# Selective scan: the product with B made in token-by-channel form and turned into PSUM, the states summed by accumulating transposes

## The reference, cut to what matters

```
xz = Z @ in_proj_w.T; x, z = split(xz)                 # 256 channels each
x = silu(causal_conv(x) + b)
dt, B, C = split(x @ x_proj_w.T)                       # 8, 16, 16 columns
dt = softplus(dt @ dt_proj_w.T + dt_proj_b)
h_t = exp(dt_t * A) * h_(t-1) + dt_t * B_t * x_t       # per channel (256) and state (16)
y_t = sum over the 16 states of h_t * C_t,  then y = (y + x * D) * silu(z)
```

## Time and profile before

| | us |
|---|---|
| median of 3 runs (1807.96 to 1814.98) | 1811.38 |
| the profiled execution, its own time | 1805.02 |
| its span in the profile | 1803.2 |
| first scan starts, last gate ends | 161.2, 943.5 |
| PE / DVE / ACT / POOL busy over the span | 1457.0 / 1317.4 / 796.5 / 563.6 |

### The profile page before, as it was taken

How to read it: one execution, slowest core, us unless ns; L and a number is a source line. 1 busy time by engine, 2 the same in 40 slices (tenths; PEclk the granted TensorE clock), 3 DMA queues, 4 the chain that set the end, 5 groups by cost and what they waited for, 6 DMA issues and landing times. The chain is left out here.

```text
span 1803.2 us, 20461 instructions
## 1 busy us (share of the span) xinstructions
PE 1457.0 (81%) x6865; PEld 867.1 (48%) x6866; DVE 1317.4 (73%) x2521; ACT 796.5 (44%) x1946; POOL 563.6 (31%) x460
## 2 busy tenths in 40 slices
PE   3897888887977775798996694412899999999998
PEld 2442333333322222366676563301576767777776
DVE  3607999999999989999980835698355555677667
ACT  4435545453555544344432365520444444444542
POOL 0006535322576652444453741000111110254100
PEclk9997989898888886899998798556899999999999
DMA  5002434344333311234455310101212111012001
GB/s 187 1 1 61 129 93 133 89 114 118 89 102 108 103 59 42 85 111 111 115 135 166 106 29 7 50 0 46 60 40 64 40 39 39 22 35 34 10 7 42
DMA packets 75998, 127.23 MB, mean 71 GB/s; under 512 B 11870, under 2 KB 38718, under 8 KB 75286
## 3 DMA queue, kind: packets, MB, share of 16 engines
q1 hardware_dynamic: 56438, 75.04, 13.8%
q0 software_dynamic: 19456, 50.88, 10.7%
HBM read 85.51 MB, written 40.37 MB: 70 GB/s over the span
## 5 line engine op out<-in xcount | busy, mean ns | idle before, releaser
L539 DVE TENSOR_TENSOR_SCAN sc_st<-sc_dA,sc_st 128x1024 f32<-128x1024 f32 x128 | 291.5, 2318 | 0.0
L1862 DVE COPY at_pT<-at_p_t 128x512 f32<-128x512 f32 (+1 forms) x192 | 109.6, 599 | 174.1 <-PE at_p_t L1756 174.1
L1143 POOL DMA_INDIRECT g_state<-xn_scratch,moe_tab x96 | 123.5, 1286 | 252.4 <-POOLq L194 141.3
L510 DVE TENSOR_TENSOR sc_st<-sc_p_b,sc_u 128x512 f32<-128x512 f32 x256 | 165.6, 682 | 41.6 <-PE sc_p_y L419 31.0
L351 ACT ACTIVATE sc_dA<-sc_dt,g_state 128x511 f32<-128x511 f32 x256 | 169.0, 709 | 27.6 <-DVE sc_st L539 26.1
L1735 PE MATMUL at_p_s<-att_xaT,at_qT 128*128 128x512 f32 (+3 forms) x512 | 173.3, 460 | 0.0
L1769 PEld LDWEIGHTS at_p_o<-at_V,at_pT 128*128 128x128 f32 x1280 | 154.0, 194 | 29.6 <-issue 28.8
L1814 ACT ACTIVATE at_pr<-at_p_s,at_nmx 128x512 f32<-128x512 f32 (+3 forms) x256 | 131.5, 529 | 64.0 <-DVE at_nmx L1840 63.9
L1174 POOL DMA_INDIRECT g_state<-r_scratch,moe_tab x96 | 114.0, 1188 | 141.6 <-PE e_bank L1273 102.0
L400 PE MATMUL sc_p_b<-sc_bc,mamba_sel 96*128 96x512 bf16 x128 | 55.6, 434 | 126.0 <-DVE sc_st L510 125.2
L1769 PE MATMUL at_p_o<-at_V,at_pT 128*128 128x128 f32 x1280 | 155.3, 277 | 1.8 <-DVE g_state L1853 1.8
(11 more groups left out here) (283 smaller groups left out, 2823.2 us busy)
## 6 DMA issues: line engine op xcount, KB each, us to landing
y_scratch<-g_state SPq DMA_DIRECT2D x24, 768.0 KB, 5.4
g_state<-W SPq DMA_DIRECT2D x48, 256.0 KB, 5.4
r_scratch<-g_state SPq DMA_DIRECT2D x16, 512.0 KB, 2.9
y_scratch<-g_state SPq DMA_DIRECT2D x24, 192.0 KB, 3.2
xn_scratch<-g_state SPq DMA_DIRECT2D x16, 256.0 KB, 2.0
g_state<-x SPq DMA_DIRECT2D x4, 512.0 KB, 5.3
g_state<-xn_scratch SPq DMA_DIRECT2D x8, 256.0 KB, 6.0
g_state<-x SPq DMA_DIRECT2D x1, 2048.0 KB, 11.6
```

The source lines that it names most:

```text
L510: ins = nc.vector.tensor_tensor(st[:, m % RS, j, :], p_b[:, :], u[:, b % 2, h, :], ALU.mult)
L539: nc.vector.tensor_tensor_scan(st[:, m % RS, :, :].rearrange("p a b -> p (a b)"), dA[:, m % 4, :, :].rearrange("p a b -> p (a b)"), st[:, ...
L1143: nc.gpsimd.indirect_dma_start(out=self.xg[:, e % 4, h, :], out_offset=None, in_=self.xn_rows, in_offset=bass.IndirectOffsetOnAxis(ap=r.ta ...
```

## The change

Per state instead of per pair (128 iterations N of `n` = 0 to 15 in `b`), with these parts:

- B is computed token by token (`b_by_token`) and u is turned (`turn_u`), so that u and B lie as tokens x channels: B is then one number per partition. `times_b` is a product with a per-partition scalar, 128x256 for each of 4 blocks of tokens: two on ACT, two on DVE, SBUF to SBUF.
- `turn_bu`: TensorE turns the 8 blocks of 128x128 into `p_u` in PSUM, one bank per half. The scans (128x512, two per state) read `p_u` there.
- `add_state`: 8 transposes (`is_transpose`, `start=False`) accumulate the finished state in `p_y`, now tokens x channels. `start_y` puts x * D there first, by products with a diagonal of D.
- `gate` is one product of 128x1024; z comes as tokens x channels from the input stage, and `turn_y` and `take_yT` turn the result back. The ReLU goes from DVE to ACT. `broadcast_b` is gone, and the work of `split_bc` and `softplus` is spread over the iterations.

The core of the diff, in the order input stage, ScalarE (from the ReLU to `take_yT`), TensorE (from `turn_bu` to the two `turn_y` at the end), VectorE:

```diff
-                    nc.scalar.activation(zT[:, e - HALF, b * L:(b + 1) * L], pj[:, n % 3, :],
+                    t = b * TB + 2 * (e - HALF)
+                    nc.scalar.activation(z[:, t:t + 2, :].rearrange("p a b -> p (a b)"), pj[:, n % 3, :],
...
+                link(nc.scalar.activation(logs[:, 1, :], logs[:, 0, :], ACT.Ln, bias=1.0))
+                nc.scalar.activation(dt[:, b % 2, h, :], p_x[:, :], ACT.Relu,
+                                     bias=w["dt_b"][:, h:h + 1]).then_inc(logs_ready, 1)
...
+            def times_b(N):
+                b, n = divmod(N, DS)
...
+                if N >= 3:
+                    act.wait_ge(bu_turned[1], N - 2)
+                for t in range(2):
+                    ins = nc.scalar.activation(bu[:, N % 3, t, :], uT[:, b % 2, t, :], ACT.Copy,
+                                               scale=BT[:, b % 2, t, n:n + 1])
+                ins.then_inc(bu_act, 1)
...
+            for N in range(STATES):
+                b, n = divmod(N, DS)
+                if N + 2 < STATES:
+                    decays(N + 2)
+                yield
+                if N + 2 < STATES:
+                    times_b(N + 2)
+                if b + 1 < B:
+                    if n == 1:
+                        softplus_logs(b + 1, 0)
+                    if n == 4:
+                        softplus_logs(b + 1, 1)
+                    if n == 6:
+                        take_BT(b + 1)
+                    if n == 7:
+                        take_uT(b + 1, 0)
+                    if n == 10:
+                        take_uT(b + 1, 1)
+                if b and n in (11, 12):
+                    take_yT(b - 1, n - 11)
...
+            def turn_bu(N, h):
+                if h == 0:
+                    pe.wait_ge(bu_act, N + 1)
+                    pe.wait_ge(bu_dve, N + 1)
+                if N:
+                    pe.wait_ge(scanned[h], N)
+                for t in range(TB):
+                    ins = nc.tensor.transpose(p_u[:, h, t * P:(t + 1) * P], bu[:, N % 3, t, h * P:(h + 1) * P],
+                                              w["ident"])
+                ins.then_inc(bu_turned[h], 1)
...
+            def add_state(N):
...
+                pe.wait_ge(hc_ready, N + 1)
+                for t in range(TB):
+                    for h in range(HALF):
+                        ins = nc.tensor.matmul(p_y[:, t, h * P:(h + 1) * P], st[:, N % 3, h, t * P:(t + 1) * P],
+                                               w["ident"], is_transpose=True, start=False,
...
+            for N in range(STATES):
+                b, n = divmod(N, DS)
+                if N + 1 < STATES:
+                    turn_bu(N + 1, 0)
...
+                yield
+                broadcast_c(N)
+                if N:
+                    add_state(N - 1)
+                if N + 1 < STATES:
+                    turn_bu(N + 1, 1)
+                yield
+            add_state(STATES - 1)
+            for h in range(HALF):
+                turn_y(B - 1, h)
...
+            def times_b(N):
...
+                for t in range(2, TB):
+                    ins = nc.vector.tensor_scalar(bu[:, N % 3, t, :], uT[:, b % 2, t, :], BT[:, b % 2, t, n:n + 1],
+                                                  None, ALU.mult)
+                ins.then_inc(bu_dve, 1)
...
+            def scan(N, h):
...
+                nc.vector.tensor_tensor_scan(st[:, N % 3, h, :], dA[:, (2 * N + h) % 6, :], p_u[:, h, :],
+                                             0.0, ALU.mult, ALU.add).then_inc(scanned[h], 1)
...
+            for N in range(STATES):
+                b, n = divmod(N, DS)
+                scan(N, 0)
+                if n == 1 and b:
+                    gate(b - 1)
+                if N:
+                    times_c(N - 1)
...
+                scan(N, 1)
+                if N + 2 < STATES:
+                    times_b(N + 2)
...
+                yield
```

More of the change, by code:

```diff
@@ L319, in copy_dt_rank @@
                 if b:
[L320 to L321 removed]
+                    act.wait_ge(u_turned, 2 * b)
+                nc.scalar.activation(dtr, p_x[96:96 + DTR, :], ACT.Copy).then_inc(dr_copied, 1)
             def softplus_logs(b, h):
@@ L325, in softplus_logs @@
                 act.wait_ge(dt_product, n + 1)
+                act.wait_ge(bc_done, b + 1)
                 if n:
[L327 to L331, removed]
-                link(nc.scalar.activation(logs[:, 0, :], lost[:, :], ACT.Exp, scale=-1.0))
@@ new lines, in take_yT, with decays @@
+            def take_yT(b, h):
+                act.wait_ge(y_turned, 2 * b + h + 1)
+                nc.scalar.activation(xT[:, h, b * L:(b + 1) * L], p_x[:, :], ACT.Copy).then_inc(yT_ready, 1)
+            def decays(N):
+                b, n = divmod(N, DS)
+                if n == 0:
+                    act.wait_ge(dt_done, 2 * b + 2)
+                for h in range(HALF):
+                    if N >= 3:
+                        act.wait_ge(scanned[h], N - 2)
+                    nc.scalar.activation(dA[:, (2 * N + h) % 6, :], dt[:, b % 2, h, :], ACT.Exp,
+                                         scale=negA[:, h, n:n + 1]).then_inc(decay_ready, 1)
@@ L339, in scalar_steps @@
             softplus_logs(0, 1)
-            act.wait_ge(cleared, 1)
+            take_BT(0)
+            take_uT(0, 0)
+            take_uT(0, 1)
+            times_b(0)
             act.wait_ge(neg_A, 1)
[L343 to L351, removed]
-                                               scale=negA[:, h, 2 * q + j:2 * q + j + 1])
-                ins.then_inc(decay_ready, 1)
@@ new lines, in gate @@
+            def gate(b):
+                dve.wait_ge(hc_used, DS * (b + 1))
+                t = slice(b * TB, (b + 1) * TB)
+                nc.vector.tensor_tensor(z[:, t, :], p_y[:, :, :], z[:, t, :], ALU.mult).then_inc(gated, 1)
+            for _ in split_bc(0):
+                pass
+            for h in range(HALF):
+                for _ in softplus(0, h):
+                    pass
+            times_b(0)
+            times_b(1)
+            for N in range(STATES):
+                b, n = divmod(N, DS)
+                scan(N, 0)
+                if n == 1 and b:
+                    gate(b - 1)
+                if N:
+                    times_c(N - 1)
+                if b + 1 < B:
+                    if n == 0:
+                        extra = split_bc(b + 1)
+                    if n == 3:
+                        extra = softplus(b + 1, 0)
+                    if n == 6:
+                        extra = softplus(b + 1, 1)
+                    if n < 9:
+                        next(extra, None)
+                scan(N, 1)
+                if N + 2 < STATES:
+                    times_b(N + 2)
+                if b + 1 < B and n < 9:
+                    next(extra, None)
+                yield
```

340 lines of the change are left out of this document (174 added, 166 removed).

## The result

| | before | after |
|---|---|---|
| median, us | 1809.67 (1807.84 to 1814.98, 4 runs) | 1863.06 (1861.79 to 1865.69, 4 runs) |
| ratio, with its 95% interval | | 1.0291 (1.0266 to 1.0317) |
| span of the profiled execution | 1803.2 | 1859.7 |

The account below looks back on a forecast made before the run. VectorE was taken to set the pace, with TensorE close behind. Start +4, first product +36, combination -36, second product +6 and end +4 gave +14, so 1825 us; the range was 1777 to 1895, the forecast's own 1800 to 1865.

Parts of the forecast that it names:

- What bounds the kernel: In the scan's three stretches VectorE sets the pace, TensorE is close behind at 85%, 76% and 93% busy, ScalarE at half.
- what TensorE does: Per state, 4 x 0.43 us of summing and a 0.22 broadcast go; 16 transposes, 1.74 us, come; batch extras add 0.55.
- the new loop: First product, 50 states: TensorE waits each state for ScalarE's product with B behind the experts' slot; 6.35 us per state, +36.
- Second product: Last 36 states: 5.03 us per state before extras, 202 us against 196.1, +6.
- Start and end: Extra turns and B by token ahead of the first scan, +4; last gate and two turns ahead of 24 remaining slots, +4.
- Prices: On VectorE, TENSOR_SCALARs at 0.26 us each, expected to show at 0.3; scans of 128x512 expected to show at 1.13 us.
- Combination: Middle 42 states: loop open, VectorE decides; savings, collisions with GpSimd and 8 for TensorE give 268 against 304.2 us, -36.
- VectorE's saving: Net 1.66 us less VectorE work per step, from cheaper products, no ReLU and a smaller gate; 35 us over the combination's 21 steps.
- Rival 1: VectorE's saving comes through in the combination, at 240 us; with shorter loops elsewhere 1777 us in all, faster; chance 0.25.
- Rival 2: More stalls: the combination gains nothing, the first product takes 6.9 us per state; 1889 us; chance 0.13.
- Rival 3: TensorE's clock falls to half because transposes do not keep it up; +480, 2290 us; chance 0.06.
- Rival 4: No loop, with ScalarE ahead of TensorE: 1655 us; chance 0.01.

Follow-up runs that it names:

- b_late: Changed kernel with ScalarE's decays of state N+2 moved behind the experts' slot, between its copies and the product with B: 2021.5 us, ratio 1.110.
- early_again: The b_early kernel run once more on another chip, beside other kernels: 1771.25 us, ratio 0.9795 to the kernel before.
- the pair with small products: GpSimd's two products per unit cut to two columns, in both kernels: changed kernel 1852.36 us, ratio 1.0135; kernel before 1797.14 us, ratio 0.9821.
- the combined version: Changed kernel with ScalarE's product with B early, the combination's slots spread, and all four blocks on ScalarE in the combination: 1719.77 us, ratio 0.9476.
- b_early: Changed kernel with ScalarE's product with B moved ahead of its decays and the experts' slot: 1826.41 us, ratio 1.0015.

## Why the prediction was wrong

- **What bounds the kernel, what TensorE does, the new loop**: right. 6.35 us per state were worked out and 317.3 / 50 = 6.35 measured; the wait was 1.49 us for 1.63 to 1.82, so the other terms were some 0.2 us too small, and that the two met exactly is luck. `b_late` and `early_again` move the stretch as the loop says (+91, -64).
- **Second product**: 202 forecast, 198.9 measured, typical states 5.10 for 5.03. On other chips the same kernel took 213.0 us there, so the closeness of the total is partly the chip's. `early_again` shows TensorE's own 170.6 us close below.
- **Start and end**: 4 and 4 forecast, 5.4 and 4.3 measured.
- **Prices**: a pair of TENSOR_SCALARs takes 0.59 us alone, 0.3 each; a scan of 128x512 is followed by the next instruction 1.13 us after its start (568.99 to 570.12). Right.
- **Combination, the failed step**: "285 - 35 - 6 + 16 = 260, and 8 for PE". It came to 312.9, 45 us more. Which instructions collide was right; how often they do, and what a collision costs beyond itself, was not. The split below is an estimate: it takes the pair with small products, from another chip, together with the first profiles.
  - *Collisions, some 21 us.* The step gave them a net +10: 16 for the TENSOR_SCALARs (1 us per unit, argued from GpSimd's pair falling "mostly beside the two immune scans") less 6. Measured: 58.8 us of the stretch with the change, 304.2 - 276.5 = 27.7 before, net 31. L604 alone was stretched by 29.5 us, 1.8 per unit where the step took 1 out of its 0 to 2.4, and each delay also left TensorE idle and then at the lower clock.
  - *VectorE's saving, 5.6 us*: 254.4 - 225.0 = 29.4 without collisions instead of 35.
  - *Waits for TensorE, some 18 us.* The step took the 19 us away and put 8 back, 11 less in all. In the pair of small-product kernels VectorE's idle time is 37.7 us with the change (262.7 - 225.0) and 22.1 before (276.5 - 254.4), 15.6 more. Some 9 of these stand in the states 51 and 91 and are not in the first profile: 15.6 + 11 - 9. In the kernel after, 28 us are waits for TensorE.
- **The total**: 1863 still lies within the 1800 to 1865 that the forecast was given, but the change is nearly four times the +14. The error is one term, the combination's; the other four together are off by 2 us.
- **Rival 1** (the saving comes through in the combination) was wrong in the change as made. It is what happens once the TENSOR_SCALARs are off VectorE there: 262.4 us in the combined version. **Rival 2** came nearest in place, wrong in its price for the first product. **Rival 3** is refuted: the granted clock was 0.96, 0.83 and 1.00, with sixteen transposes per state. "TensorE: Matmul & The Clock Gate" of the Trainium skill, Part 4, says that the full clock does not engage for transposes, as they don't count as activity in the same way. The trace differs: four of them took 0.60 us at full clock. Every stretch here also holds ordinary products, so what transposes count for by themselves is not shown. **Rival 4** had no chance as the order stood; with the order changed 255.7 and 253.6 us came for the first product.

What stays open: 32 to 51 us of VectorE's idle time in the combination, in every version of the changed order (47.6 in the best). The order of TensorE's slots moved the stretch by 4 and 5 us, half the columns of its experts' slots by 6. In the best version 25.0 us of it are waits for ScalarE's rstd and 15.7 for the C row; no run took that chain apart.

## What to carry to other kernels

When work moves from an operand in PSUM to SBUF on both sides, price it beside whatever GpSimd does then, near the worst case, and ask what waits behind it. In these traces a cheap 0.3 us TENSOR_SCALAR, a product of two SBUF operands and a tiny norm step were all held for about a whole GpSimd product; what read PSUM never was. An instruction put behind a slot of another program inherits that slot's waits, even on an engine that is half idle: put it ahead of the slot first. That alone took 4 to 5% off: a loss of 3% (on some chips 4.5%) became a gain of 2% (on some chips nothing). Split work between engines per stretch, by who has time there, not once for the whole loop.

## What was not expected of the hardware

- An f32 TENSOR_SCALAR of 128x256, 0.30 us alone, lasted up to 3.15 us beside a GpSimd product of 2.35 us; scans and products with an operand in PSUM kept their 1.22 and 1.20 us. The scans of the kernel before, with both operands in SBUF, took 2409 ns in the combination and 2270 with the small products; four of the 42 took over 2.7 us, the longest 4.37.
- The same program had different times on different chips, beyond what the kernel before had (its medians lay between 1805.5 and 1831.4): `b_early` took 192.5 us for the second product and `early_again` 176.1, the unedited changed kernel 198.9 and 213.0, in ratio 1.029 and 1.045. The kernel before took 196.1 and, with small products, 195.9. In those traces the changed kernels stand longer at the borders of the experts' kinds of slots (state 91 takes 9.72 us for 3.94). A later landing of the gathered rows could do this; the traces of those chips do not show landings, and it was not tried.
- Less work for TensorE at the same pace lowered its granted clock: 0.83 to 0.76 in the kernel before with half the columns. The time it saved was still 12 us of the stretch.
